# Last attention of a four-layer block: scores first in each step, three places for the weights, and the sums of weights inverted while compact

## The chip, the cores and the metric

The kernel runs on one core of a Trainium2 chip. The metric is the device time of one execution in microseconds (us). The core has five engines, each with its own instruction queue, worked off in order: PE (TensorE, matrix products; PEld are its weight loads), DVE (VectorE), ACT (ScalarE), POOL (GpSimd) and SP, which here only issues DMA transfers. Engines wait for one another on semaphores. SBUF is the on-chip memory of 128 partitions; PSUM, eight banks of 512 float32 per partition (`ps` in the code), takes PE's results.

## The reference, cut to what matters

Four layers of gated cross-attention and feed-forward act on 32 batches of 56 queries, with 1500 context rows of 96 features each. The change lies in the attention of the last layer, called L3:

```python
# 32 batches, 56 queries of 128 features, 1500 keys of 96 features, 16 heads of 8
q = (query @ Wq + bq); k = (key_value @ Wk + bk); v = (key_value @ Wv + bv)
attn = jnp.einsum('bhqd,bhkd->bhqk', q, k) * scale
attn = jnp.clip(attn, -CLAMP, CLAMP)              # CLAMP = 10000
attn = jax.nn.softmax(attn, axis=-1)
attn = jnp.where(jnp.any(jnp.isnan(attn)), 1.0 / Nkv, attn)
x = jnp.einsum('bhqk,bhkd->bqhd', attn, v)
return x @ Wo + bo
```

## The kernel before

All of L3's attention is `clipped_pass`. The 32 batches go through a pipeline in software: batches 0 to 7 and 24 to 31 are written out, 8 to 23 are two turns of a loop over eight batches (`batches`). A batch is 12 steps (`KT`), k = 0 to 11, one for each tile of 125 keys; a tile has 896 columns, 16 heads times 56 queries. Every engine has its own `body(b)`, and the order of the calls in it is the order of its queue.

**Step k of batch b** does, for the tile k of this batch, the last part of its work, and for later ones the first parts:

- PE: `weigh(b, k)` (line 1942, 8 products of the weights `P` with the values, summed in bank 4), then `chunks` (line 1910, 2 products of 500 columns for the maximum of batch b+1 or b+2, bank pair 6 and 7), then `score(b, k + 2)` (line 1929, 8 products, bank pair 0 and 1 or 2 and 3), then `fifth_bank(b, k)`.
- DVE: `chunk_max` (line 2109, the maximum over the two chunks), then `clip_tile(b, k + 2)` (line 2126), which clips scores from PSUM into a place of `P`. `P` has two places, so the clip of tile n waits until tile n-2 is weighed. In k = 2 two small operations follow the maximum (lines 2114 and 2117).
- ACT: `Exp` of tile n in place (line 2075), and ahead of it what the fifth bank holds (`empty(misc(b, n - 2))`) and, at n = 5, 7 and 8, a third of `second_of_keys` (line 2031).

**The fifth bank** of PSUM (index 5) is shared by all side work, in an order that the table `MISC` sets: keys of batch b+3 in three parts (k = 0, 1, 2; PE line 1844, emptied by ACT lines 2016 and 2020), at k = 3 in even batches the sums of the weights of the two batches before (`spread_sums`, line 1868) and in odd ones the projection (`project`, line 1877), at k = 6 the turned maximum of batch b+1 (`turn`, lines 1858 and 1859), at k = 7 to 10 the values of batch b+1 (line 1851, emptied by ACT line 2008). Before a new tenant PE waits until the last one is emptied (`used_earlier`, `emptied`).

**Sums.** `copy_sums` (ACT line 2043) brings a batch's bank 4, 128x224, to `UE`. In each even batch PE spreads the sums of the weights over the rows of their head (result 128x448), and DVE inverts them in two halves of 224 columns, at k = 3 and 4 (`invert`, line 2139). POOL multiplies (`norm`, lines 1806 and 1808).

**Keys.** They are split into three bfloat16 parts on ACT and POOL (lines 2016, 1770, 2031, 1775), and when the last third is ready SP issues six DMAs of 375 KB (`place_keys`, line 1708) into one of four buffers `KS`. `chunks` of batch b+2 needs them at step k = 3 of batch b. The turned maximum goes out and back by DMA (`place_max`, lines 1713 to 1717), ahead of the keys in SP's queue, and the first clip of the next batch waits for it.

The lines that set the order of a step before are these:

```python
for k in range(KT):                       # PE
    weigh(b, k)
    chunks(of, c)
    score(b, k + 2)
    fifth_bank(b, k)
for k in range(KT):                       # DVE
    chunk_max(of, c)
    clip_tile(b, k + 2)
    if b.r % 2 == 0 and (b - 2).there() and k in (3, 4):
        invert(b - 2, k - 3)
```

Of the kernel before, what the change touches and what calls it, by code (L numbers as in the profile page):

```python
# [15 lines left out]
BF16 = mybir.dt.bfloat16  # L16
# [17 lines left out]
DH = 8  # L34
# [1490 lines left out]
class Eight(Batch):  # L1525
# [12 lines left out]
                "u_copied", "sums_spread", "sums_inverted", "u_normed", "seen", "projected", "out_copied"]  # L1538
# [51 lines left out]
def clipped_pass(core, L, S, src, bo, scale, clip, ok, ctx):  # L1590
# [6 lines left out]
    QS = [sb(f"qs{s}", [128, HQ + 16], BF16) for s in range(8)]  # L1597
# [24 lines left out]
    def queries(b):  # L1622
        return QS[b.r % 8][:, 0:HQ].rearrange("p (m j q) -> p m j q", j=2, q=NQ)
# [24 lines left out]
    MISC = {0: ("keys", 0), 1: ("keys", 1), 2: ("keys", 2), 3: ("pair", 0), 6: ("turn", 0),  # L1648
            7: ("values", 0), 8: ("values", 1), 9: ("values", 2), 10: ("values", 3)}

    def misc(b, k):
# [3 lines left out]
        kind, n = MISC[k]  # L1655
        if kind == "pair":
            kind = "project" if b.r % 2 else "sums"
        of = {"values": b + 1, "keys": b + 3, "turn": b + 1, "sums": b - 2, "project": b - 3}[kind]
# [4 lines left out]
    def emptied(kind, n, of):  # L1663
# [26 lines left out]
    with nc.Block() as block:  # L1690
        @block.sync
        def _(sp):
# [55 lines left out]
        def _(pool):  # L1748
# [8 lines left out]
            def place_queries(b):  # L1757

                if b.turn is not None or b.r >= 8:
                    pool.wait_ge(S["scored"], b.lin(12, -84))  # L1760
                for u, (_, part) in enumerate(PRODUCTS):
                    for j in range(2):
# [3 lines left out]
                                       ).then_inc(S[f"q_in{b.r % 8}"], 16)  # L1766
# [35 lines left out]
            def norm(b):  # L1802
                pool.wait_ge(S["sums_inverted"], b.lin(1, 2))
# [23 lines left out]
            pool.wait_ge(S["q_zeroed"], 8)  # L1827
# [7 lines left out]
            place_queries(first + 3)  # L1835
# [4 lines left out]
        def _(pe):  # L1840
# [21 lines left out]
            def of_head(t, j):  # L1862
                return t.rearrange("p (s r j q) -> p (s r) j q", s=2, j=2, q=NQ)[:, :, j, :]
# [1815 lines left out]
```

## Time and profile before

| | before |
| --- | --- |
| median of 3 runs | 4645.66 us |
| lowest and highest | 4640.62 and 4651.19 us |
| the profiled execution | 4638.98 us, of it 4637.4 us span |
| L3's attention, steps of all batches | about 3580 to 4533 us of the span |
| busy in these 953 us: DVE, PE, ACT, POOL | 866, 810, 583, 465 us |
| granted TensorE clock in them | 0.94 of full |

The stage fills a fifth of the span. No engine is busy in all of it, but DVE and PE are so in over four fifths, and which of them ends a step last differs from step to step; so the rows below show single steps. A row of the timeline begins with its start in us from the span's start, then how long it took, the engine, the line, the operation and, in brackets, how long the engine was idle before it and who released it.

### The profile page before, as it was taken

To read this page: it belongs to the slowest core of one execution; us is meant where nothing else is said; L and a number is where in the kernel's file an instruction comes from. 1 tells how busy PE (TensorE), PEld (TensorE's weight loads), DVE (VectorE), ACT (ScalarE), POOL (GpSimd) and SP (SyncE) were. 2 spreads that over 40 slices of the span, in tenths; PEclk is the share of its full clock that TensorE was granted. 3 is DMA by queue.
4 is the path that set the end of the run, shared out by engine and by line. 5 is a ranking of instruction groups with operands and counts; after the bars stand their busy time and mean duration, and the time that the engine had idled before them with its cause. 6 is when DMAs were issued, how large, how long until landed. Compare 5 with 4: busy or idle time off the path is not lost. (4 is left out here: it accounts for less than half of the span.)

```text
span 4637.4 us, 86565 instructions
## 1 busy us (share of the span) xinstructions
PE 3793.5 (82%) x32862; PEld 2469.2 (53%) x32862; DVE 2849.1 (61%) x3552; ACT 2051.5 (44%) x2875; POOL 1444.6 (31%) x1905
## 2 busy tenths in 40 slices
PE   7389889871748999998999996599595888888885
PEld 7156556640425666664666663277332555555553
DVE  8666555643336555535555543577546999989993
ACT  7166666640212334332343342366222666656652
POOL 0264445303132323212223210022005555545520
PEclk9689999985868999997999997799796999989997
DMA  6166666723532323212333320110004665555630
GB/s 168 38 150 147 146 136 142 157 70 133 196 71 53 88 84 83 80 46 70 85 87 87 83 59 15 42 48 28 17 0 105 136 137 134 127 131 130 136 87 14
DMA packets 197065, 434.62 MB, mean 94 GB/s; under 512 B 45707, under 2 KB 98877, under 8 KB 196588
## 3 DMA queue, kind: packets, MB, share of 16 engines
q1 hardware_dynamic: 122196, 338.87, 28.9%
q0 software_dynamic: 38912, 47.06, 4.7%
q10 hardware_dynamic: 35616, 43.97, 3.5%
q8 instruction: 236, 3.87, 0.4%
q14 instruction: 105, 0.86, 0.1%
HBM read 244.72 MB, written 32.67 MB: 60 GB/s over the span
## 5 line engine op out<-in xcount | busy, mean ns | idle before, releaser
L1446 DVE TENSOR_REDUCE L_mp<-ps 112x2 f32<-112x1000 f32 x384 | 458.2, 1199 | 507.7 <-PE ps L1268 504.1
L1305 PE MATMUL ps<-L_p,L_cn 125*97 125x448 f32 x1536 | 639.2, 538 | 0.0
L1429 ACT ACTIVATE L_p<-ps 125x896 f32<-125x896 f32 x384 | 352.2, 917 | 612.5 <-PE ps L1293 540.5
L2109 DVE TENSOR_REDUCE L_mp<-ps 112x2 f32<-112x1000 f32 x384 | 456.6, 1193 | 71.4 <-PE ps L1910 48.3
L2075 ACT ACTIVATE L_p<-L_p 125x896 f32<-125x896 f32 x384 | 365.1, 951 | 254.9 <-DVE L_p L2126 254.6
L911 ACT ACTIVATE L_p<-ps,rk 125x896 f32<-125x896 f32 x384 | 385.8, 1005 | 161.9 <-PE ps L789 142.9
L2126 DVE SCALAR_TENSOR_TENSOR L_p<-ps,xn 125x896 f32<-125x896 f32 x384 | 415.1, 1082 | 26.6 <-DMA xn<-L_low 17.9
L1291 PE MATMUL ps<-L_qh,L_ch 97*125 97x448 f32 x768 | 385.6, 502 | 13.9 <-DMA L_qh<-L_mc 13.9
L1305 PEld LDWEIGHTS ps<-L_p,L_cn 125*97 125x97 f32 x1536 | 250.4, 163 | 205.8 <-issue 165.9
L1942 PE MATMUL ps<-L_p,L_vs 125*18 125x112 f32 x6144 | 233.6, 272 | 113.7 <-ACT L_p L2075 101.6
L1910 PE MATMUL ps<-L_ks,L_qs 96*128 96x500 bf16 x768 | 248.6, 410 | 46.2 <-DVE L_mp L2109 23.7
L1292 PE MATMUL ps<-L_ql,L_ch 96*125 96x448 f32 x768 | 283.9, 370 | 0.0
L1293 PE MATMUL ps<-L_qh,L_cl 96*125 96x448 f32 x768 | 282.2, 367 | 0.0
L1268 PE MATMUL ps<-L_cr,L_qb 96*112 96x500 f32 x768 | 269.0, 437 | 13.3 <-DVE L_mp L1446 7.0
L802 PE MATMUL ps<-L_p,L_vs 125*32 125x112 f32 x6144 | 240.1, 275 | 30.9 <-ACT L_p L911 13.0
L1942 PEld LDWEIGHTS ps<-L_p,L_vs 125*18 125x18 f32 x6144 | 131.5, 100 | 235.9 <-ACT L_p L2075 191.5
L1929 PEld LDWEIGHTS ps<-L_qs,L_ks 128*128 128x128 bf16 x3072 | 199.8, 102 | 101.8 <-issue 21.4
L789 PE MATMUL ps<-L_qs,L_ks 128*128 128x112 bf16 x3072 | 230.3, 221 | 6.1 <-issue 6.1
L1929 PE MATMUL ps<-L_qs,L_ks 128*128 128x112 bf16 x3072 | 226.9, 220 | 4.5 <-DMA L_qs<-L_mt 4.5
L710 POOL DMA_DIRECT2D L_qs<-L_q_part x384 | 216.9, 573 | 9.7 <-DVEq L1018 6.8
L1764 POOL DMA_DIRECT2D L_qs<-L_q_part x384 | 214.2, 565 | 8.1 <-issue 5.5
L1220 POOL TENSOR_TENSOR L_un<-L_ue,L_rb 96x896 f32<-96x896 f32 x32 | 67.2, 2101 | 453.9 <-DMA L_rb<-L_den 453.9
(518 smaller groups left out, 7285.5 us busy)
## 6 DMA issues: line engine op xcount, KB each, us to landing
L_ks<-L_k_part SPq DMA_DIRECT2D x288, 375.0 KB, 9.7
L_ks<-L_k_first SPq DMA_DIRECT2D x96, 375.0 KB, 7.2
moe_w<-in_L_w SPq DMA_DIRECT2D x64, 512.0 KB
L_cn<-in_ctxN SPq DMA_DIRECT2D x32, 568.4 KB
cs_ct<-in_ctxT SPq DMA_DIRECT2D x32, 562.5 KB, 4.2
L_raw<-in_ctxT SPq DMA_DIRECT2D x32, 562.5 KB
L_cr<-in_ctxT POOLq DMA_DIRECT2D x32, 562.5 KB, 4.9
L_ch<-in_ctxT POOLq DMA_DIRECT2D x32, 562.5 KB, 4.4
```

The source lines that it names most:

```text
L911: nc.scalar.activation(P[0:KP, n % 2, :].rearrange("p (a n) -> p a n", a=2), SB[n % 2][0:KP], ACT.Exp, scale=rk[:, bass.ds(b.lin(KT, n), 1 ...
L1291: nc.tensor.matmul(SB[n % 2][:, a, :], CH[s][:, k], QH[s][:, q], start=True, stop=False)
L1292: nc.tensor.matmul(SB[n % 2][:, a, :], CH[s][0:DC, k], QL[s][:, q], start=False, stop=False)
L1293: mm = nc.tensor.matmul(SB[n % 2][:, a, :], CL[s][:, k], QH[s][0:DC, q], start=False, stop=True)
L1305: mm = nc.tensor.matmul(U[:, a, :], CN[s][:, j, :], P[:, n % 2, a * HALF:(a + 1) * HALF], start=(j == 0), stop=(j == KT - 1))
L1429: nc.scalar.activation(two(P[:, n % 2, :]), SB[n % 2], ACT.Exp).then_inc(S["exped"].sem, 1)
L1446: nc.vector.tensor_reduce(mp[:, 2 * k:2 * k + 2], ps[0:TT, bank:bank + 2, 0:500], AX.X, ALU.max).then_inc(S["chunk_maxed"].sem, 1)
L1929: mm = nc.tensor.matmul(SB[n % 2][:, m // 4, m % 4 * 2 * NQ:(m % 4 + 1) * 2 * NQ] .rearrange("p (j q) -> p j q", j=2), KS[b.r % 4][:, k0:k ...
L1942: mm = nc.tensor.matmul(ps[32 * g:32 * g + VW, 4, c:c + 2 * NQ], VS[b.r % 2][:, j, m, :], P[0:KP, j % 2, m * 2 * NQ:(m + 1) * 2 * NQ], sta ...
L2075: nc.scalar.activation(two(P[0:KP, n % 2, :]), two(P[0:KP, n % 2, :]), ACT.Exp).then_inc(S["exped"], 1)
L2109: nc.vector.tensor_reduce(mp[:, 2 * c:2 * c + 2], ps[0:TT, CB[pair], 0:500], AX.X, ALU.max).then_inc(S["chunk_maxed"], 1)
L2126: nc.vector.scalar_tensor_tensor(out=two(P[0:KP, n % 2, :]), in0=SB[n % 2][0:KP], scalar=0.0, in1=two(LB[0:KP, b.r % 2, :]), op0=ALU.min, ...
```

## The change

Parts, all within `clipped_pass`:

1. PE's step begins with `score(b, k + 2)`, and `weigh`, `chunks` and `fifth_bank` follow. DVE's step begins with `clip_tile(b, k + 2)`, and `chunk_max` follows.
2. `P` has three places instead of two; to pay for them `QS`, the queries' buffers, go from eight to four, and queries are placed three batches ahead instead of four.
3. ACT empties the fifth bank one tile later (ahead of tile n what step n-3 put there, not n-2), and the first third of `second_of_keys` moves from n = 5 to 6.
4. The sums are first picked out compactly: `pick_sums` (PE, k = 3, 4 products with 4 columns) gives 112x16, `invert` is one reciprocal of 112x16, `widen` (ACT, ahead of tile 6) repeats it to two tiles 112x256, `spread_sums` (PE, k = 5, 4 products with 112 columns) brings them to 128x448, and `take_sums` (ACT, ahead of tile 8) copies that to `RD` for POOL.
5. The turned maximum moves from k = 6 to k = 4.

```diff
-    QS = [sb(f"qs{s}", [128, HQ + 16], BF16) for s in range(8)]
+    QS = [sb(f"qs{s}", [128, HQ + 16], BF16) for s in range(4)]
-    P = sb("p", [128, 2, HQ])
+    P = sb("p", [128, 3, HQ])
+    RC = sb("rc", [2 * NQ, 4, 4])
-    MISC = {0: ("keys", 0), 1: ("keys", 1), 2: ("keys", 2), 3: ("pair", 0), 6: ("turn", 0),
+    MISC = {0: ("keys", 0), 1: ("keys", 1), 2: ("keys", 2), 3: ("pair", 0), 4: ("turn", 0), 5: ("spread", 0),
...
+            def pick_sums(b):
+                pe.wait_ge(S["u_copied"], b.lin(1, 2))
+                for c in range(4):
+                    mm = nc.tensor.matmul(ps[0:2 * NQ, 5, 4 * c:4 * c + 4], UE[:, c // 2, c % 2 * 2 * NQ:][:, 0:2 * NQ],
+                                          core.ident[:, DH:128:32], start=True, stop=True)
+                mm.then_inc(S["sums_picked"], 1)
             def spread_sums(b):
-                pe.wait_ge(S["u_copied"], b.lin(1, 2))
-                for j in range(2):
-                    mm = nc.tensor.matmul(of_head(ps[:, 5, 0:2 * QV], j), core.sum_row[:, j, :],
-                                          of_head(UE[:, :, :].rearrange("p s n -> p (s n)"), j),
-                                          start=True, stop=True)
+                pe.wait_ge(S["sums_widened"], twice_half_of(b, 2))
+                for c in range(4):
+                    mm = nc.tensor.matmul(ps[:, 5, c * 2 * NQ:(c + 1) * 2 * NQ],
+                                          wide(c // 2)[:, c % 2 * 128:(c % 2 + 1) * 128],
+                                          core.ident[0:2 * NQ, 0:2 * NQ], start=True, stop=True)
...
             def body(b):            # PE
                 for k in range(KT):
+                    if k + 2 < KT:
+                        score(b, k + 2)
+                    elif (b + 1).there():
+                        score(b + 1, k + 2 - KT)
                     weigh(b, k)
                     of, c = chunk_of(b, k)
                     if of.there():
                         chunks(of, c)
-                    if k + 2 < KT:
-                        score(b, k + 2)
-                    elif (b + 1).there():
-                        score(b + 1, k + 2 - KT)
                     fifth_bank(b, k)
...
+            def widen(b):           # ACT
+                act.wait_ge(S["sums_inverted"], half_of(b, 1))
+                if b.turn is not None or b.r:
+                    act.wait_ge(S["u_normed"], b.lin(1, 0))
+                    act.wait_ge(S["projected"], half_of(b, 0))
+                for n in range(2):
+                    nc.scalar.activation(wide(n).rearrange("p (c g d) -> p c g d", c=2, g=4),
+                                         RC[:, 2 * n:2 * n + 2, :].unsqueeze(3).to_broadcast([2 * NQ, 2, 4, 32]),
+                                         ACT.Copy).then_inc(S["sums_widened"], 1)
...
-                    if n >= 2:
-                        empty(misc(b, n - 2))
+                    if n >= 3:
+                        empty(misc(b, n - 3))
                     elif (b - 1).there():
-                        empty(misc(b - 1, n + 10))
-                    for at, c in ((5, 0), (7, 1), (8, 2)):
+                        empty(misc(b - 1, n + 9))
+                    if n == 6 and b.r % 2 == 0 and (b - 2).there():
+                        widen(b - 2)
+                    for at, c in ((6, 0), (7, 1), (8, 2)):
...
             def clip_tile(b, n):    # DVE
-                if b.turn is not None or b.r or n >= 2:
-                    dve.wait_ge(S["weighed"], b.lin(12, n - 1))
+                if b.turn is not None or b.r or n >= 3:
+                    dve.wait_ge(S["weighed"], b.lin(12, n - 2))
...
-                nc.vector.reciprocal(RD[:, s, :], ps[:, 5, s * QV:(s + 1) * QV]).then_inc(S["sums_inverted"], 1)
+                nc.vector.reciprocal(RC[:, :, :].rearrange("p c g -> p (c g)"), ps[0:2 * NQ, 5, 0:16]
+                                     ).then_inc(S["sums_inverted"], 1)
             def body(b):            # DVE
                 for k in range(KT):
-                    of, c = chunk_of(b, k)
-                    if of.there():
-                        chunk_max(of, c)
                     if k + 2 < KT:
                         clip_tile(b, k + 2)
                     elif (b + 1).there():
                         clip_tile(b + 1, k + 2 - KT)
-                    if b.r % 2 == 0 and (b - 2).there() and k in (3, 4):
-                        invert(b - 2, k - 3)
+                    of, c = chunk_of(b, k)
+                    if of.there():
+                        chunk_max(of, c)
+                    if b.r % 2 == 0 and (b - 2).there() and k == 3:
+                        invert(b - 2)
```

DVE's queue in steps 2 to 5 of an even batch, before (L2109 is the maximum, L2126 the clip, L2114 and L2117 the two small operations that end a batch's maximum):

```order
L2109 TENSOR_REDUCE L_mp<-ps 112x2
L2114 TENSOR_REDUCE L_mu<-L_mp 112x8
L2117 TENSOR_SCALAR L_mc<-L_mu 112x8
L2126 SCALAR_TENSOR_TENSOR L_p<-ps,xn 125x896
L2109 TENSOR_REDUCE L_mp<-ps 112x2
L2126 SCALAR_TENSOR_TENSOR L_p<-ps,xn 125x896
L2139 RECIPROCAL L_rd<-ps 128x224
L2109 TENSOR_REDUCE L_mp<-ps 112x2
L2126 SCALAR_TENSOR_TENSOR L_p<-ps,xn 125x896
L2139 RECIPROCAL L_rd<-ps 128x224
```

The same place after the change (L2152 is the maximum, L2169 the clip):

```order
L2152 TENSOR_REDUCE L_mp<-ps 112x2
L2157 TENSOR_REDUCE L_mu<-L_mp 112x8
L2160 TENSOR_SCALAR L_mc<-L_mu 112x8
L2169 SCALAR_TENSOR_TENSOR L_p<-ps,xn 125x896
L2152 TENSOR_REDUCE L_mp<-ps 112x2
L2182 RECIPROCAL L_rc<-ps 112x16
L2169 SCALAR_TENSOR_TENSOR L_p<-ps,xn 125x896
L2152 TENSOR_REDUCE L_mp<-ps 112x2
L2169 SCALAR_TENSOR_TENSOR L_p<-ps,xn 125x896
```

Clips and maxima alternate as they did; two reciprocals of 224 columns have become one of 16.

PE's queue from step 2 of an even batch, before (L1844 keys, L1942 weigh, L1910 chunks, L1929 score, L1868 the sums spread):

```order
L1844 MATMUL ps<-L_ck,L_wk 128x500
L1942 MATMUL ps<-L_p,L_vs 18x112 x8
L1910 MATMUL ps<-L_ks,L_qs 128x500 x2
L1929 MATMUL ps<-L_qs,L_ks 128x112 x8
L1868 MATMUL ps<-L_ue,sum_row 128x4x56 x2
L1942 MATMUL ps<-L_p,L_vs 18x112 x8
L1910 MATMUL ps<-L_ks,L_qs 128x500 x2
L1929 MATMUL ps<-L_qs,L_ks 128x112 x8
L1942 MATMUL ps<-L_p,L_vs 18x112 x8
```

And after (L1857 keys, L1948 score, L1961 weigh, L1929 chunks, L1878 the sums picked, L1871 and L1872 the turned maximum, L1885 the inverted sums spread):

```order
L1857 MATMUL ps<-L_ck,L_wk 128x500
L1948 MATMUL ps<-L_qs,L_ks 128x112 x8
L1961 MATMUL ps<-L_p,L_vs 18x112 x8
L1929 MATMUL ps<-L_ks,L_qs 128x500 x2
L1878 MATMUL ps<-ident,L_ue 112x4 x4
L1948 MATMUL ps<-L_qs,L_ks 128x112 x8
L1961 MATMUL ps<-L_p,L_vs 18x112 x8
L1929 MATMUL ps<-L_ks,L_qs 128x500 x2
L1871 MATMUL ps<-ident,L_st 24x112
L1872 MATMUL ps<-ident,L_st 8x112
L1948 MATMUL ps<-L_qs,L_ks 128x112 x8
L1961 MATMUL ps<-L_p,L_vs 18x112 x8
```

The scores now stand behind the fifth bank's work and ahead of the weighing, where they stood behind the chunks.

## Rows read from the trace of the kernel before

**Rows 1.** The stage: us, busy PE, PEld, DVE, ACT, POOL; clock, DMA share, GB/s

```profile
3580.00:4533.00 953.00, 810.35 (x11074) 517.19 (x11078) 866.07 (x839) 583.16 (x877) 464.75 (x802) 0.94 0.56 126
```

**Rows 2.** Timeline of DVE: clip of tile 1 in batches 2, 13, 14, 30

```profile
3640.54 1.08 DVE L2126 SCALAR_TENSOR_TENSOR L_p<-ps,xn 125x896 f32<-125x896 f32 x1
...
3973.86 1.08 DVE L2126 SCALAR_TENSOR_TENSOR L_p<-ps,xn 125x896 f32<-125x896 f32 x1
...
4001.23 1.08 DVE L2126 SCALAR_TENSOR_TENSOR L_p<-ps,xn 125x896 f32<-125x896 f32 x1
...
4491.02 1.08 DVE L2126 SCALAR_TENSOR_TENSOR L_p<-ps,xn 125x896 f32<-125x896 f32 x1
```

**Rows 3.** Timeline, batch 14, steps 3 to 7: reciprocals and what waits

```profile
4011.83 1.08 DVE L2126 SCALAR_TENSOR_TENSOR L_p<-ps,xn 125x896 f32<-125x896 f32 x1
...
4012.83 1.55 DVE L2139 RECIPROCAL L_rd<-ps 128x224 f32<-128x224 f32 x1
...
4015.35 1.07 DVE L2126 SCALAR_TENSOR_TENSOR L_p<-ps,xn 125x896 f32<-125x896 f32 x1
...
4016.45 0.95 ACT L2075 ACTIVATE L_p<-L_p 125x896 f32<-125x896 f32 x1 [2.56 <-DVE L_p L2126]
...
4018.99 1.01 PE L1910 MATMUL ps<-L_ks,L_qs 96*128 96x500 bf16 x2 [0.59 <-DVE L_mp L2109]
...
4021.06 0.95 PE L1942 MATMUL ps<-L_p,L_vs 125*18 125x112 f32 x16
...
4024.61 0.58 PE L1942 MATMUL ps<-L_p,L_vs 125*18 125x112 f32 x16
```

**Rows 4.** Granted clock and DMA share in two stretches of batch 14, columns as in rows 1

```profile
4000.00:4004.00 4.00, 3.06 (x49) 1.78 (x51) 3.72 (x5) 2.29 (x4) 0.00 (x0) 1.00 1.05 190
...
4020.00:4024.00 4.00, 4.00 (x39) 2.71 (x37) 3.20 (x3) 2.77 (x5) 1.85 (x2) 0.51 0.03 6
```

**Rows 5.** What DVE waited for in the stage: total, times, longest

```profile
DVE L_mp L2109 <- PE ps L1910: 44.4, 75, 2.0
DVE L_p L2126 <- DMA xn<-L_low: 17.9, 10, 10.5
...
DVE L_mp L2109 <- issue: 7.9, 1, 7.9
```

**Rows 6.** Timeline, batch 14, a step with keys in the fifth bank

```profile
4003.85 0.59 ACT L2016 ACTIVATE L_k_first<-ps 128x500 bf16<-128x500 f32 x1 [0.56 <-PE ps L1844]
...
4004.34 0.58 ACT L2020 ACTIVATE L_k_full<-ps 128x500 f32<-128x500 f32 x1
...
4006.08 0.58 PE L1942 MATMUL ps<-L_p,L_vs 125*18 125x112 f32 x16
...
4007.03 0.56 PE L1929 MATMUL ps<-L_qs,L_ks 128*128 128x112 bf16 x8
...
4007.42 1.06 PE L1844 MATMUL ps<-L_ck,L_wk 97*128 97x500 f32 x2
...
4008.42 0.58 PE L1942 MATMUL ps<-L_p,L_vs 125*18 125x112 f32 x16
```

**Rows 7.** Two rows that price new operations: a DVE group, a projection

```profile
L2117 DVE TENSOR_SCALAR L_mc<-L_mu 112x8 f32<-112x8 f32 x32 | 5.5, 172 | 1.1
...
4043.51 1.10 PE L1877 MATMUL ps<-L_un,L_woe 128*128 128x112 f32 x8
```

**Rows 8.** The keys' DMAs placed in batch 13, and the chunk that waits

```profile
3992.05 1.30 SPq L1708 DMA_DIRECT2D L_ks<-L_k_first  x2
...
4010.08 0.59 PE L1910 MATMUL ps<-L_ks,L_qs 96*128 96x500 bf16 x2 [1.09 <-DMA L_ks<-L_k_part]
```

**Rows 9.** Timeline of the last steps and of the end of the stage

```profile
4526.22 1.09 DVE L2126 SCALAR_TENSOR_TENSOR L_p<-ps,xn 125x896 f32<-125x896 f32 x1 [0.80 <-PE ps L1929]
...
4529.46 1.09 DVE L2126 SCALAR_TENSOR_TENSOR L_p<-ps,xn 125x896 f32<-125x896 f32 x1 [0.79 <-PE ps L1929]
...
4535.13 2.97 DVE L2139 RECIPROCAL L_rd<-ps 128x224 f32<-128x224 f32 x2 [3.21 <-PE ps L1868]
```

More of the change, by code:

```diff
@@ L1655, in misc @@
         kind, n = MISC[k]
+        if kind == "spread" and b.r % 2:
+            return None
         if kind == "pair":
             kind = "project" if b.r % 2 else "sums"
-        of = {"values": b + 1, "keys": b + 3, "turn": b + 1, "sums": b - 2, "project": b - 3}[kind]
+        of = {"values": b + 1, "keys": b + 3, "turn": b + 1, "sums": b - 2, "spread": b - 2, "project": b - 3}[kind]
         if not of.there():
@@ L1671, in emptied @@
         if kind == "sums":
-            return S["sums_inverted"], of.lin(1, 2)
+            return S["sums_inverted"], half_of(of, 1)
+        if kind == "spread":
+            return S["sums_copied"], half_of(of, 1)
         return S["out_copied"], half_of(of, 1)
@@ L1679, in half_of, with wide, twice_half_of @@
         return 4 * b.turn + (b.r // 2 + c)
+    def wide(n):
+        return (RD, UN)[n][0:2 * NQ, :, :].rearrange("p s n -> p (s n)")[:, 0:256]
+    def twice_half_of(b, c):
+        if b.turn is None:
+            return b.r // 2 * 2 + c
+        return 8 * b.turn + (b.r // 2 * 2 + c)
     def used_earlier(b, k):
@@ L1757, in place_queries @@
             def place_queries(b):
-                if b.turn is not None or b.r >= 8:
-                    pool.wait_ge(S["scored"], b.lin(12, -84))
+                if b.turn is not None or b.r >= 4:
+                    pool.wait_ge(S["scored"], b.lin(12, -36))
                 for u, (_, part) in enumerate(PRODUCTS):
@@ L1810, in body @@
             def body(b):
-                if (b + 4).there():
-                    place_queries(b + 4)
+                if (b + 3).there():
+                    place_queries(b + 3)
                 if (b + 3).there():
@@ L1834, in _ @@
             place_queries(first + 2)
-            place_queries(first + 3)
             batches(pool, body)
@@ L1894, in fifth_bank @@
                 if kind == "sums":
+                    pick_sums(of)
+                if kind == "spread":
                     spread_sums(of)
@@ L1999, in _ @@
             pe.wait_ge(*emptied("project", 0, last - 2))
+            pick_sums(last)
             spread_sums(last)
@@ L2043, in copy_sums, with take_sums @@
                 nc.scalar.activation(UE[:, b.r % 2, :], ps[:, 4, 0:QV], ACT.Copy).then_inc(S["u_copied"], 1)
+            def widen(b):
[7 more added lines that the diff above has]
+                                         ACT.Copy).then_inc(S["sums_widened"], 1)
+            def take_sums(b):
+                act.wait_ge(S["sums_spread"], half_of(b, 1))
+                if b.turn is not None or b.r:
+                    act.wait_ge(S["u_normed"], b.lin(1, 0))
+                nc.scalar.activation(RD[:, :, :].rearrange("p s n -> p (s n)"), ps[:, 5, 0:2 * QV], ACT.Copy
+                                     ).then_inc(S["sums_copied"], 1)
             def out(b):
@@ L2059, in empty @@
                     copy_turned(of)
+                if kind == "spread":
+                    take_sums(of)
                 if kind == "project":
@@ L2074, in body @@
                     act.wait_ge(S["clipped"], b.lin(12, n + 1))
-                    nc.scalar.activation(two(P[0:KP, n % 2, :]), two(P[0:KP, n % 2, :]), ACT.Exp
+                    nc.scalar.activation(two(P[0:KP, n % 3, :]), two(P[0:KP, n % 3, :]), ACT.Exp
                                          ).then_inc(S["exped"], 1)
@@ L2100, in make_parts @@
                 dve.wait_ge(S["q_made"], 1)
-                qf, rest = (t[:, :, :].rearrange("p s n -> p (s n)") for t in (P, LB))
+                qf, rest = (t[:, :, :].rearrange("p s n -> p (s n)") for t in (P[:, 0:2, :], LB))
                 link(nc.vector.tensor_scalar(qf.rearrange("p (c n) -> p c n", c=NCH), ps[:, 0:NCH, 0:CH],
@@ L2123, in clip_tile @@
                 dve.wait_ge(S["scored"], b.lin(12, n + 1))
-                if b.turn is not None or b.r or n >= 2:
-                    dve.wait_ge(S["weighed"], b.lin(12, n - 1))
-                nc.vector.scalar_tensor_tensor(out=two(P[0:KP, n % 2, :]), in0=SB[n % 2][0:KP], scalar=0.0,
+                if b.turn is not None or b.r or n >= 3:
+                    dve.wait_ge(S["weighed"], b.lin(12, n - 2))
+                nc.vector.scalar_tensor_tensor(out=two(P[0:KP, n % 3, :]), in0=SB[n % 2][0:KP], scalar=0.0,
                                                in1=two(LB[0:KP, b.r % 2, :]), op0=ALU.min, op1=ALU.max
@@ L2167, in _ @@
             batches(dve, body)
-            for s in range(2):
-                invert(Eight(None, B - 2), s)
+            invert(Eight(None, B - 2))
             dve.wait_ge(S["u_normed"], B)
```

30 lines of the change are left out of this document (15 added, 15 removed).

## The prediction

> **What bounds the kernel now.** I read first the span by stretches, then DVE's timeline over whole batches, then single steps. In the stage DVE is busy 866 of 953 us and PE 810 [rows 1]; ACT with 583 and POOL with 465 have room. So a step ends with DVE or PE, and the question is which, step by step. One step of DVE is a clip and a maximum. Where nothing else happens they follow one another without idle time; batch 13, an odd one, runs from its clip of tile 1 at 3973.86 to that of batch 14 at 4001.23, in 27.37 us [rows 2]. Less 0.35 us for the two small operations of step 2 (0.17 each [rows 7]) that is 2.25 us a step. Over batches 2 to 29 the same measure is 4491.02 - 3640.54 = 850.5 us for 28 batches [rows 2]. In it lies one stop of 7.9 us in which DVE waited for nothing that the profile names ("issue", once) [rows 5]; it stands at the turn of the loop, the change does not touch it, and I leave it in both times. The rest, 842.6 us, is 30.1 us a batch, 2.7 more than batch 13 took. If every batch ran like batch 13, 28 x 2.72 = 76.2 us would go. That is the room I look into.
>
> **Where the room is.** In even batches DVE inverts two halves of 224 columns. One reciprocal takes 1.55 us, and it is not hidden: the clips at 4011.83 and 4015.35 stand 3.52 us apart [rows 3], against 2.25 us for a step with nothing in it, and the next pair is alike. Meanwhile ACT waits 2.56 us for its clip and PE 0.59 us for the maximum [rows 3]. So two reciprocals cost an even batch 2.5 us at once. Behind them the chunks take 1.01 us for 2 products instead of 0.59 [rows 3, 8] and the granted clock falls to 0.51 of full, the lower of its two levels (1.2 of 2.4 GHz), from 1.00 [rows 4]: ahead of it PE had had 1.7 us of work (0.58 + 0.59 + 0.56 [rows 6, 8]) in each of two steps of 3.5 us, and now its steps are longer than DVE's. The remaining excess is in waits of DVE for the chunks (44.4 us in 75 waits, the low clock among their causes) and for the returned maximum (17.9 us, of it 10.5 in the first batch) [rows 5]. In the one odd batch shown none of this happens, though its queue is else the same; this is why I take an odd batch as the model of what is left.
>
> **The change part by part.** All against the profiled execution of 4638.98 us.
>
> *The reciprocal.* It goes from 2 x 224 to 16 columns. Its price lies between 0.17 us, the group of 8 columns [rows 7], and the 16/224 of 1.55 on top of that, 0.28; I take 0.2, since the 8 columns already carry what is fixed. It waits for `pick_sums`, 4 products of 4 columns, which end while the maximum of step 3 still runs: nothing on the path. Batch 13 has no reciprocal, so against 76.2 us 14 even batches pay 14 x 0.2 = 2.8 us.
>
> *Widening, spreading, taking.* On PE, `spread_sums` is four products with 112 columns, as the projection is: 1.10 us [rows 7]; with the other three groups that makes a step of about 2.4 us, 0.15 over DVE's 2.25, so 14 x 0.15 = 2.1 us. From below it is nothing, since step 6 has no tenant and gives it back. On ACT, two copies of 256 columns cost under 0.59 each, the price of 500 [rows 6], say 0.4, and taking 448 columns about 0.55: 1.4 us in 2 batches, spread over two steps in which ACT now waits for its clip. POOL's `norm` gets its sums at tile 8 instead of step 4; it comes behind the thirds of the keys, which end about then anyway, so it costs nothing as long as those do.
>
> *Scores first, three places.* The order on DVE is as before, clip and maximum in turn, and PE does the same products a batch. In steps with side work in the fifth bank PE is itself full (a keys step is 4006.08 to 4008.42, 2.34 us, with no idle time [rows 6]), and no order changes that. So in full batches I give this nothing beyond batch 13's time. At the end of the stage it counts: from batch 30, step 3, on there are no chunks, and two steps take 4529.46 - 4526.22 = 3.24 us [rows 9], because clip, exponential, weighing and scores form a ring over two places. With three places and scores ahead of the weighing the ring opens, and a step is bound by DVE's 1.09 or PE's 0.58 + 0.56. Of 18 steps some 10 have no tenant: 10 x (1.62 - 1.12) = 5.0 us. Batch 30's own two reciprocals save 2.5 us, and 0.4 for the clock behind them. At the very end 2.97 us of reciprocals [rows 9] and a 1 us spreading turn into picking, 0.2, widening, 1.10 and taking, about 3.5 us in all: 0.4 us. Together 8.3 us.
>
> *ACT one tile later.* Here the change can lose. Before a new tenant PE waits until ACT has emptied the bank. For keys that now means: exponential of tile k+1, then two copies, 4003.85 to 4004.92, 1.07 us [rows 6], and only then the next 1.06 us of products and 0.6 of scores. Counted from DVE's clip in step 1: ACT is through with tile 2 at -0.2, with the copies at 0.9; keys to 1.95, scores to 2.6 us. DVE would be ready at 2.25, and the step takes 2.34 now. So one step in each batch grows by 0.26 us, 28 x 0.26 = 7.3 us. Step 2 hides the same behind the two small operations, step 3 behind a tenant that starts later; values are copied faster and pass. The bounds are 0 (the phase between PE and DVE takes it up) and three such steps, 22 us.
>
> *The maximum turned two steps earlier, four buffers of queries.* SP hands out the returned maximum before the keys, and the clip of the next batch has some 1 to 2 us more: the 7.4 us of waits after the first batch mostly end. They are not in batch 13, so this is already in the room. Queries are still placed more than a batch ahead of their use; nothing.
>
> *What does not go.* Batches also differ by small stalls, keys that land late above all; I leave 0.1 us a batch, 2.8 us.
>
> **The sum.** 76.2 - 2.8 - 2.1 - 7.3 - 2.8 = 61.2 us, with 8.3 at the end 69.5 us. From 4638.98 this gives 4569.5 us. The median of the three runs was 4645.66, 6.7 us above the profiled execution, and the new median should stand alike: **4576 us**.
>
> **The rivals.**
>
> *The keys' DMA becomes the bound.* The keys of batch 13 were handed out from 3992.05, and the chunk that needs them started at 4010.08, having waited 1.09 us [rows 8]: 18 us, with the DMA engines full (share 1.05 [rows 4]). After the change I put the last third at 8.9 us behind step 3's clip (three steps of 2.25, then ACT and POOL with 2.2 us), so keys allow a period of 27 us; DVE needs 27.6. Against: the margin is positive. For: it is 0.6 us, and I take one burst for all. Each us beyond costs 28 us; at one, 4604 us.
>
> *ACT holds up the fifth bank in more steps.* If keys, projection and values each lose 0.2 to 0.3 us, 1 us a batch, the time is again 4604 us.
>
> *The low clock stays.* If steps 4 to 6 of even batches, where PE works 1.7 of 2.25 us, are enough to bring it down without the reciprocals, about 2 us in 14 batches remain: 28 us, 4604 us. Against it is batch 13, which has such steps at full clock.
>
> *More than I allow.* Without the losses of ACT and spreading, and with stalls gone, 12 to 15 us more go: 4562 us.
>
> *Slower than before.* One mechanism: the clock. PE's waits for ACT in steps 1 and 3 are new idle times, in every batch and not in every second. Should they bring the clock down, a step costs 3.55 us (4021.06 to 4024.61 [rows 3]) instead of 2.25, 1.3 more. The gain is used up when 69.5 / 1.3 = 53 of the 336 steps run so in addition, 16%; the granted clock in the stage would fall from 0.94 [rows 1] to under 0.90. At 25% of the steps, 84 of them, the time is 4576 + 84 x 1.3 = 4685 us. Against it: a keys step of 2.6 us still holds 2.3 us of PE's work, where ahead of the fall two steps of 3.5 us held 1.7 each. The Trainium skill (TensorE: Matmul & The Clock Gate, section "A second HAM failure mode: psum-queue depth-cycling") reports a kernel that cycled through PSUM banks and left PE idle briefly between groups so often that the clock went up and down, at a price in throughput. This trace agrees in part: the fall in batch 14 came behind idle times, but odd batches with shorter ones stay at full clock.
>
> *The change does not free DVE.* Excluded by the 3.52 us, in which DVE has no idle time.
>
> **How the numbers follow.** Forecast 62% (4576, within 12 either way); more 7%; keys' DMA 9%; ACT 9%; low clock stays 8%; slower 4%; a mixture that nets to nothing 1%. The range, 4552 to 4608 us, takes in the deeper gain and the three at 4604. A measurement of this kernel tells about 0.2%, 9 us, from no change: faster 0.94, same 0.02, slower 0.04.
>
> **What would show it.** Even and odd batches alike, both about 27.6 us; clips 2.2 to 2.5 us apart around the small reciprocal, which takes 0.2; the granted clock in the stage at 0.97 or more; ACT no longer waiting 2.5 us. The keys step 1 to 2 grows to about 2.6 us if the ACT term is right. The last steps come at 1.1 us. The DMA rival would show as chunks released by the keys in most batches, the ACT rival as keys and values products released by its copies with DVE idle after, the clock rival as chunks of 1.01 us. A mean batch above 28.5 us would make the prediction wrong.

## The result, and the profile after

The changed kernel takes 4528.81 us (median of 4 runs, 4514.69 to 4530.06), the kernel before, beside it, 4645.25 us. That is 116 us less; the ratio is 0.974, 95% interval 0.9723 to 0.9757. Forecast were 4576 us, 69 us less, with a range down to 4552. The sign was right; the gain is 1.7 times the forecast one, and the time lies outside the range.

The profiled execution has a span of 4528.5 us, 108.9 less than before. Measured as in [rows 2], from the clip of tile 1 in batch 2 to that in batch 30, the steps take 749.1 us instead of 850.5: 101.4 of the 108.9 us are there. The sum had 61.2 for them. It had 8.3 for the end of the stage, where 4.3 us went: the clips of batches 30 and 31 are through 4.9 us sooner, and the work behind the last clip takes 0.6 us longer. Batches 0 and 1, which the sum left out, gave 6.1 us, and the work outside the stage took 2.8 us more. So the error is in the full batches. Two equal stretches of the stage show the pace; the first line of numbers is after, the second before (columns as in [rows 1]):

```profile
3640.00:4300.00 660.00, 611.31 (x8749) 414.13 (x8748) 636.38 (x654) 461.70 (x740) 390.46 (x668) 0.99 0.67 151
```

```profile
3640.00:4300.00 660.00, 565.65 (x7525) 357.84 (x7529) 601.56 (x584) 404.28 (x615) 340.18 (x580) 0.93 0.58 133
```

DVE is now busy 96% of the time, and the granted clock is 0.99. An even batch takes 26.29 us and an odd one 26.21, almost without spread but for batches 15 and 16 at the turn of the loop (34.6 and 32.3 us). The forecast had 27.6 for both, because it took the 27.37 us of batch 13 [rows 2] for what is left when the reciprocals go.

The groups of the stage after, 3580 to 4440 us, as in [rows 7] (busy, mean ns, idle before):

```profile
L2152 DVE TENSOR_REDUCE L_mp<-ps 112x2 f32<-112x1000 f32 x363 | 432.0, 1190 | 2.6 <-PE ps L1929 2.6
L2169 DVE SCALAR_TENSOR_TENSOR L_p<-ps,xn 125x896 f32<-125x896 f32 x384 | 414.5, 1081 | 40.5 <-PE ps L1948 29.1 <-DMA xn<-L_low 11.0
L2116 ACT ACTIVATE L_p<-L_p 125x896 f32<-125x896 f32 x384 | 364.7, 950 | 228.0 <-DVE L_p L2169 227.4
```

The maximum waits 2.6 us for its chunks where it waited 44.4 [rows 5], and of the 40.5 us ahead of the clip 11.0 are the first batch and 8.3 + 3.2 the stop at the turn of the loop. No instruction of the stage waited for the keys' DMAs any more.

**How a step ran before and runs now.** Timeline of the kernel before, batch 15, steps 4 and 5, with no tenant (no side work) in the fifth bank:

```profile
4046.81 1.08 DVE L2126 SCALAR_TENSOR_TENSOR L_p<-ps,xn 125x896 f32<-125x896 f32 x1
...
4047.81 1.19 DVE L2109 TENSOR_REDUCE L_mp<-ps 112x2 f32<-112x1000 f32 x1
4047.93 0.95 ACT L2075 ACTIVATE L_p<-L_p 125x896 f32<-125x896 f32 x1 [1.42 <-DVE L_p L2126]
...
4048.91 1.08 DVE L2126 SCALAR_TENSOR_TENSOR L_p<-ps,xn 125x896 f32<-125x896 f32 x1
4048.93 0.58 PE L1942 MATMUL ps<-L_p,L_vs 125*18 125x112 f32 x16 [0.87 <-ACT L_p L2075]
4049.44 0.60 PE L1910 MATMUL ps<-L_ks,L_qs 96*128 96x500 bf16 x2
...
4050.07 1.20 DVE L2109 TENSOR_REDUCE L_mp<-ps 112x2 f32<-112x1000 f32 x1
...
4051.19 1.08 DVE L2126 SCALAR_TENSOR_TENSOR L_p<-ps,xn 125x896 f32<-125x896 f32 x1
```

DVE seems busy without a gap, yet the second maximum starts 1.16 us after its clip and the first 1.00. The second one waited: the chunks end at 4049.44 + 0.60 = 4050.04, and it starts at 4050.07. The records of two successive DVE instructions overlap by 0.08 us (1.08 long, 1.00 apart), and idle time as short as the other 0.08 us here is not printed, so a wait of 0.16 us shows neither as idle time nor as a releaser. From this follows a ring, a chain of waits that comes back to where it began, through DVE, ACT and PE: clip at 4046.81, exponential at 4047.93, weighing at 4048.93, chunks, maximum at 4050.07, clip at 4051.19. That is 4.38 us for two steps, 2.19 a step, where DVE alone would take 2.10. The same in the changed kernel, batch 14:

```profile
3974.57 1.08 DVE L2169 SCALAR_TENSOR_TENSOR L_p<-ps,xn 125x896 f32<-125x896 f32 x1
...
3974.71 0.60 PE L1929 MATMUL ps<-L_ks,L_qs 96*128 96x500 bf16 x2 [0.39 <-DVE L_mp L2152]
...
3975.57 1.19 DVE L2152 TENSOR_REDUCE L_mp<-ps 112x2 f32<-112x1000 f32 x1
...
3975.89 0.56 PE L1948 MATMUL ps<-L_qs,L_ks 128*128 128x112 bf16 x8
...
3976.37 0.58 PE L1961 MATMUL ps<-L_p,L_vs 125*18 125x112 f32 x16
...
3976.68 1.08 DVE L2169 SCALAR_TENSOR_TENSOR L_p<-ps,xn 125x896 f32<-125x896 f32 x1
...
3976.89 0.60 PE L1929 MATMUL ps<-L_ks,L_qs 96*128 96x500 bf16 x2
```

Clip to maximum is 1.00 us, maximum to clip 1.11: 2.10 us a step, and this is a step with values in the fifth bank, which took 2.23. Here PE waits for DVE (0.39), not the other way. From then on PE is slower than DVE as long as the fifth bank has values: its chunks are 2.18 us apart (3974.71, 3976.89), the clips 2.11 (3974.57, 3976.68). PE enters these steps with a lead, loses some 0.07 us in each, and has it again from steps without a tenant, where its chunks come as close as 1.89 us apart. The clip at 3976.68 starts while the tile two before it is still being weighed (3976.37 to 3976.95), which needs the third place.

### The profile page after: what moved, and what is told of

Same layout as the page of the kernel before. It is cut to its first block and busy times, and to the rows that moved or that the text cites. A ratio compares the mean times of both kernels' runs of the same rounds, so it can differ in the third digit from the quotient of the medians.

```text
span 4528.5 us, 87018 instructions
## 1 busy us (share of the span) xinstructions
PE 3764.9 (83%) x33054; PEld 2482.9 (55%) x33054; DVE 2775.7 (61%) x3532; ACT 2053.0 (45%) x2923; POOL 1442.9 (32%) x1905
## 5 line engine op out<-in xcount | busy, mean ns | idle before, releaser
L2152 DVE TENSOR_REDUCE L_mp<-ps 112x2 f32<-112x1000 f32 x384 | 455.4, 1190 | 6.5 <-PE ps L1929 6.5
L2169 DVE SCALAR_TENSOR_TENSOR L_p<-ps,xn 125x896 f32<-125x896 f32 x384 | 414.5, 1081 | 40.5 <-PE ps L1948 29.1
L1929 PE MATMUL ps<-L_ks,L_qs 96*128 96x500 bf16 x768 | 236.2, 392 | 62.4 <-DVE L_mp L2152 50.6
L802 PE MATMUL ps<-L_p,L_vs 125*32 125x112 f32 x6144 | 240.8, 275 | 32.2 <-ACT L_ue L895 19.9
L1948 PEld LDWEIGHTS ps<-L_qs,L_ks 128*128 128x128 bf16 x3072 | 190.2, 99 | 90.2 <-issue 54.0
L789 PE MATMUL ps<-L_qs,L_ks 128*128 128x112 bf16 x3072 | 228.8, 220 | 6.9 <-issue 6.9
L1948 PE MATMUL ps<-L_qs,L_ks 128*128 128x112 bf16 x3072 | 216.5, 214 | 14.7 <-DVE L_p L2169 6.5
L1961 PE MATMUL ps<-L_p,L_vs 125*18 125x112 f32 x6144 | 223.7, 263 | 1.4 <-ACT L_p L2116 0.9
L789 PEld LDWEIGHTS ps<-L_qs,L_ks 128*128 128x128 bf16 x3072 | 166.1, 101 | 77.9 <-issue 70.7
```

The source lines that it names most:

```text
L789: mm = nc.tensor.matmul(SB[n % 2][:, m // 4, m % 4 * 2 * NQ:(m % 4 + 1) * 2 * NQ] .rearrange("p (j q) -> p j q", j=2), KS[b.r % 3][:, k0:k ...
L1948: mm = nc.tensor.matmul(SB[n % 2][:, m // 4, m % 4 * 2 * NQ:(m % 4 + 1) * 2 * NQ] .rearrange("p (j q) -> p j q", j=2), KS[b.r % 4][:, k0:k ...
L2152: nc.vector.tensor_reduce(mp[:, 2 * c:2 * c + 2], ps[0:TT, CB[pair], 0:500], AX.X, ALU.max).then_inc(S["chunk_maxed"], 1)
L2169: nc.vector.scalar_tensor_tensor(out=two(P[0:KP, n % 3, :]), in0=SB[n % 2][0:KP], scalar=0.0, in1=two(LB[0:KP, b.r % 2, :]), op0=ALU.min, ...
```

## The experiments

All times are medians beside runs of the kernel before on the same chip, and the ratio is to these. "Odd" and "even" are the median batches among 2 to 29 of the profiled execution, clip of tile 1 to clip of tile 1; all kernels keep the computation whole. The edits below are cut to the lines that matter, with calls shortened.

| run | us | ratio, 95% interval | odd, even batch | clock 3640 to 4300 |
| --- | --- | --- | --- | --- |
| before | 4645.25 | 1 | 27.8, 32.6 | 0.93 |
| after | 4528.81 | 0.974, 0.9723 to 0.9757 | 26.2, 26.3 | 0.99 |
| dve_order | 5029.80 | 1.0831, 1.081 to 1.0853 | 43.3, 42.6 | 0.80 |
| pe_order | 4631.81 | 0.9968, 0.9956 to 0.9981 | 27.2, 31.9 | 0.94 |
| both_orders | 4656.91 | 1.0034, 1.0019 to 1.0049 | 28.1, 32.2 | 0.93 |
| small_sums | 4588.46 | 0.9877, 0.986 to 0.9895 | 28.0, 28.4 | 0.98 |
| both_orders_small_sums | 4611.55 | 0.9923, 0.99 to 0.9946 | 28.6, 29.2 | 0.97 |
| small_sums_three_places | 4598.67 | 0.9909, 0.989 to 0.9927 | 28.1, 28.4 | 0.98 |
| after_two_places | 4603.09 | 0.9912, 0.9894 to 0.993 | 28.2, 28.6 | 0.99 |
| after_wide_sums | 4592.96 | 0.989, 0.9869 to 0.991 | 26.5, 30.1 | 0.94 |
| after_late_turn | 4647.37 | 1.0012, 0.9997 to 1.0026 | 30.8, 30.7 | 0.91 |
| after_again | 4529.92 | 0.9758, 0.974 to 0.9775 | 26.2, 26.3 | 0.99 |
| after_early_empty | 4514.30 | 0.9727, 0.9707 to 0.9748 | 25.9, 26.0 | 0.99 |
| early_empty_again | 4511.59 | 0.9721, 0.9704 to 0.9738 | 25.9, 26.0 | 0.99 |

**The sums alone.** The kernel before with part 4 only; the spreading at step 5, the turned maximum left at 6.

```diff
-    MISC = {..., 3: ("pair", 0), 6: ("turn", 0),
+    MISC = {..., 3: ("pair", 0), 5: ("spread", 0), 6: ("turn", 0),
-                    if b.r % 2 == 0 and (b - 2).there() and k in (3, 4):
-                        invert(b - 2, k - 3)
+                    if b.r % 2 == 0 and (b - 2).there() and k == 3:
+                        invert(b - 2)
```

> The kernel before with only the sums changed (picked, inverted as 112x16, widened, spread at step 5, taken by ACT); order, places and the turned maximum at step 6 stay. If the forecast's reading of the reciprocals was right, even batches come down from 32.3 to 27.5 to 28.0 us and odd ones stay at 27.4 to 27.7: 14 x 4.5 + 3 = 66 us less, about 4579 us, and the granted clock in the stage rises from 0.94 to 0.97 or more. If the low clock does not come from the reciprocals, about 38 us less and a clock of 0.95.

It took 4588.46 us, 56 less. Even batches fell from 32.6 to 28.4 us, odd ones stayed at 28, and the clock rose to 0.98:

```profile
3640.00:4300.00 660.00, 581.96 (x8165) 379.11 (x8164) 609.20 (x610) 440.64 (x688) 363.77 (x620) 0.98 0.62 142
```

So the forecast's reading of the reciprocals holds, the clock included, with 56 instead of 66 us; between 3640 and 4300 us DVE's waits for the chunks (30.1 us) and for the returned maximum (7.5 us) remain. What is left, 60 us, the forecast had given almost nothing.

**DVE's order alone.**

```diff
-                    chunk_max(of, c)                # DVE
-                    clip_tile(b, k + 2)
+                    clip_tile(b, k + 2)
+                    chunk_max(of, c)
```

> The kernel before with one edit: in DVE's step the clip of tile k+2 stands ahead of the maximum of step k; PE's order, two places of weights and the wide reciprocals stay. Theory A (a ring through DVE's order: clip n, exponential n, weighing n, chunks n, maximum n, clip n+2; 1.08 + 0.04 + 0.95 + 0.05 + 0.51 + 0.60 + 0.03 + 1.12 = 4.38 us in two steps, 2.19 a step): the ring is opened by this edit alone, an odd batch falls from 27.4 to about 26.5 us, the maximum follows the clip after 1.00 instead of 1.11 to 1.22 us; some 25 us less than the kernel before. Theory B (PE's order alone makes the step shorter, since the scores move behind the fifth bank's work): no change within 5 us, odd batches stay at 27.4.

385 us slower. I had followed the ring of two steps and overlooked that this edit closes one within a single step. Its timeline, in steps with keys:

```profile
4145.86 0.60 PE L1910 MATMUL ps<-L_ks,L_qs 96*128 96x500 bf16 x2
4146.30 0.56 PE L1929 MATMUL ps<-L_qs,L_ks 128*128 128x112 bf16 x8
...
4146.89 1.09 DVE L2126 SCALAR_TENSOR_TENSOR L_p<-ps,xn 125x896 f32<-125x896 f32 x1 [1.09 <-PE ps L1929]
...
4147.90 1.19 DVE L2109 TENSOR_REDUCE L_mp<-ps 112x2 f32<-112x1000 f32 x1
...
4149.15 0.60 PE L1910 MATMUL ps<-L_ks,L_qs 96*128 96x500 bf16 x2 [0.88 <-DVE L_mp L2109]
```

Chunks wait for the last maximum, scores stand behind the chunks, the clip waits for the scores and the maximum stands behind the clip: 4149.15 - 4145.86 = 3.29 us in a step at full clock, and 3.9 to 4.05 in steps at the lower clock level. Neither theory foresaw it.

**PE's order alone.**

```diff
-                    weigh(b, k); chunks(of, c); score(b, k + 2)     # PE
+                    score(b, k + 2); weigh(b, k); chunks(of, c)
```

> The kernel before with one edit: in PE's step the scores of tile k+2 stand first, ahead of weighing and chunks; DVE's order and all else stay. Theory A: the ring through the maximum stays, odd batches 27.2 us or more, no gain in full batches; only the last steps without chunks gain up to 5 us. Theory B: most of what dve_order does not give, odd batches 26.5 us, some 25 us less.

13 us less, and odd batches of 27.19 us. Theory A is right in that steps without a tenant stay at 2.19: the ring through the maximum is untouched. It is not right that full batches gain nothing: 10.5 of the 13 us are there (840.0 instead of 850.5 from batch 2 to 30), in steps with keys (2.28 instead of 2.34) and with values (2.17 to 2.21 instead of 2.23), where PE does the same products in less time.

**Both orders.**

> The kernel before with both new orders (scores first on PE, clip first on DVE), but two places of weights, eight query buffers, the fifth bank emptied as before and the wide reciprocals. Theory A: like dve_order and 5 us more at the end, about 30 us less than the kernel before, even batches still 4 to 5 us longer than odd ones. If the third place is needed for the new order, nothing is gained here, since the clip of tile n+2 waits until tile n is weighed and now comes half a step earlier.

12 us slower. Of what was expected the last sentence came true: DVE's clip is now released by the weighing. Its waits between 3640 and 4300 us, total, times and longest:

```profile
DVE L_p L2126 <- PE ps L1942: 36.5, 62, 1.8
DVE L_p L2126 <- DMA xn<-L_low: 14.2, 15, 1.9
```

**Both orders and the sums.**

> The kernel before with both new orders and the new sums, but two places of weights, eight query buffers, the fifth bank emptied as before and the maximum turned at step 6. The orders alone gained nothing (both_orders: odd batches 28.1 us). If sums and orders are independent, even batches fall to 28.3 us: 57 us less than both_orders, about 4600 us. If the orders only pay once no reciprocal stands in DVE's queue, 4560 us or less.

45 us less than both_orders, about what the sums save alone (56). The orders pay nothing with either kind of sums, so it is not the reciprocals alone that held them back. Both kernels still turn the maximum at step 6.

**The third place taken away from the changed kernel.**

```diff
-    P = sb("p", [128, 3, HQ])
+    P = sb("p", [128, 2, HQ])
...
-                if b.turn is not None or b.r or n >= 3:
-                    dve.wait_ge(S["weighed"], b.lin(12, n - 2))
+                if b.turn is not None or b.r or n >= 2:
+                    dve.wait_ge(S["weighed"], b.lin(12, n - 1))
```

> The changed kernel with two places of weights instead of three. Theory: in the changed kernel the clip of tile k+2 starts while tile k is still being weighed (3987.26 against 3987.05 to 3987.63), so with two places it must wait for the weighing, and maximum, chunks, tenant, scores, weighing, clip form a ring of two steps: 1.19 + 0.04 + 0.44 + 0.88 + 0.50 + 0.62 + 1.00 = 4.67 us with values in the fifth bank, 2.33 a step instead of 2.10, and more with keys. About 1.5 us a batch, some 42 us more than the changed kernel, 4571 us. Rival: the place only matters at the end of the stage, under 8 us more.

74 us more than the changed kernel, more than the 42 of the theory, by the mechanism named; 59 of them are in the steps of batches 2 to 29:

```profile
DVE L_p L2169 <- PE ps L1961: 56.8, 117, 7.6
```

```profile
3984.64 0.58 PE L1961 MATMUL ps<-L_p,L_vs 125*18 125x112 f32 x16
...
3985.36 1.09 DVE L2169 SCALAR_TENSOR_TENSOR L_p<-ps,xn 125x896 f32<-125x896 f32 x1 [0.33 <-PE ps L1961]
```

(The clip's start lies 0.14 us behind the modelled end of the weighing at 3985.22.) Odd batches take 28.2 us, 2 us more, where I had 1.5: steps with values alternate between 2.5 and 2.15 us as worked out, and those with keys take 2.6.

**The third place alone.** small_sums with three places and four query buffers, old order.

> The run small_sums (4588 us) with three places of weights and four query buffers added, old order on PE and DVE. Theory: with the old order the clip of tile n+2 stands behind the maximum of step n, which waits for the chunks, which stand behind the weighing of tile n; so the place is free by then anyway and the third one gains nothing in full batches: odd batches stay at 27.6 to 28.1 us, 4588 us within 6. Rival: the third place alone is what was worth 75 us in after_two_places, then 4540 us or less.

4598.67 us against 4588.46, measured on different chips and 4 us beyond the 6 expected; the steps of batches 2 to 29 take 806.6 us against 804.3. So with the old order the third place is worth nothing in full batches. The orders and the place gain only together, and, as after_late_turn shows below, only with the early turn.

**The wide reciprocals put back into the changed kernel.**

```diff
-    MISC = {..., 3: ("pair", 0), 4: ("turn", 0), 5: ("spread", 0),
+    MISC = {..., 3: ("pair", 0), 5: ("turn", 0),
-                        invert(b - 2)
+                        invert(b - 2, k - 3)        # k = 3 and 4
```

> The changed kernel with the old sums (spread at step 3, two reciprocals of 128x224 at steps 3 and 4), the maximum turned at step 5. The reciprocals cost 14 x 2.7 = 38 us in even batches. If the low clock behind them comes from them whatever the order, another 14 x 1.5 = 20 us, together about 4588 us, and chunks of 1.01 us appear in even batches only; if it came from the old order, 4568 us.

64 us more than the changed kernel, 5 us from the first theory. The clock falls to 0.94 with the new order too, and scores of 0.95 us, at the lower level, stand right behind the second reciprocal:

```profile
3941.35 1.55 DVE L2138 RECIPROCAL L_rd<-ps 128x224 f32<-128x224 f32 x1
...
3941.49 0.60 PE L1909 MATMUL ps<-L_ks,L_qs 96*128 96x500 bf16 x2 [1.89 <-DVE L_mp L2108]
...
3943.21 0.95 PE L1928 MATMUL ps<-L_qs,L_ks 128*128 128x112 bf16 x8
```

It also turns the maximum one step later, and odd batches wait about 1 us for its return; between 3640 and 4300 us that is 10.5 us in 13 waits, so some 0.4 us a batch, about 12 of the 64 us, belong to that.

**The maximum turned late.**

```diff
-    MISC = {..., 4: ("turn", 0), 5: ("spread", 0),
+    MISC = {..., 5: ("spread", 0), 6: ("turn", 0),
```

> The changed kernel with the maximum turned at step 6 instead of 4. In after_wide_sums (step 5) odd batches wait 1.0 us for the returned maximum, at step 4 nothing is waited for. If each step of delay of 2.1 us goes straight to the first clip of the next batch, this costs 3.1 us a batch, 28 x 3.1 = 87 us over the changed kernel: 4615 us. If there is slack in the return, 30 us or less.

118 us more than the changed kernel: the whole gain. The wait for the return takes 58.2 us in 21 batches between 3640 and 4300 us, and behind it comes a second cost:

```profile
DVE L_p L2169 <- DMA xn<-L_low: 58.2, 21, 4.1
```

```profile
4014.08 1.09 DVE L2169 SCALAR_TENSOR_TENSOR L_p<-ps,xn 125x896 f32<-125x896 f32 x1 [2.78 <-DMA xn<-L_low]
...
4016.34 0.76 PE L1929 MATMUL ps<-L_ks,L_qs 96*128 96x500 bf16 x2 [2.54 <-DVE L_mp L2152]
...
4018.66 1.02 PE L1929 MATMUL ps<-L_ks,L_qs 96*128 96x500 bf16 x2
```

PE stands idle for 2.5 us, then its scores take 0.95 us and the chunks 1.02, the lower level, so that a batch loses more behind the wait: 2.3 us in batch 13 (steps of 3.60 and 3.31 instead of 2.10 and 2.51), 0.5 in batch 14 and 1.4 on average. The expectation had the first cost, 87 us, without the second.

**ACT empties the bank as early as before.**

```diff
-                    if n >= 3:
-                        empty(misc(b, n - 3))
+                    if n >= 2:
+                        empty(misc(b, n - 2))
...
```

> The changed kernel with ACT emptying the fifth bank ahead of tile n what step n-2 put there, as the kernel before does. Theory A (the forecast's term for ACT): the stall of 0.40 us between the clips of steps 1 and 2 goes, 9 us less than the changed kernel, about 4520 us. Theory B: the exponentials now wait behind products that are made late in the step, weighing and chunks wait for them, and steps with tenants grow: 10 us more or worse.

4514.30 us, 14.5 less than the changed kernel had. To be sure of so little, both ran again side by side:

> The changed kernel once more, as the partner of early_empty_again on the same chip: 4515 to 4531 us, ratio to the kernel before 0.974.

> The changed kernel with the fifth bank emptied one tile earlier (as after_early_empty, a second time beside after_again). The step from 1 to 2 took 2.18 us in it instead of 2.50, so 28 x 0.33 = 9 us less than after_again, and 2 us more at the ends: 4515 us when after_again has 4526. If the 14 us between the first measurements were a matter of the chip, no difference.

4529.92 and 4511.59 us, 18 us apart. Theory A holds: the clips of steps 1 and 2 are 2.18 us apart instead of 2.50, and nothing is lost elsewhere. In the changed kernel, batch 14, the second clip waits for its scores:

```profile
3960.97 1.08 DVE L2169 SCALAR_TENSOR_TENSOR L_p<-ps,xn 125x896 f32<-125x896 f32 x1
...
3963.47 1.09 DVE L2169 SCALAR_TENSOR_TENSOR L_p<-ps,xn 125x896 f32<-125x896 f32 x1 [0.32 <-PE ps L1948]
```

In after_early_empty the clip no longer has a releaser:

```profile
3925.29 1.08 DVE L2169 SCALAR_TENSOR_TENSOR L_p<-ps,xn 125x896 f32<-125x896 f32 x1
...
3927.47 1.09 DVE L2169 SCALAR_TENSOR_TENSOR L_p<-ps,xn 125x896 f32<-125x896 f32 x1
```

The 0.32 us a batch make 9 us in 28 batches; the steps of batches 2 to 29 gave 13.9 (749.1 against 735.2 us). The other 5 are at the turn of the loop, where batches 15 and 16 together take 66.9 us in the changed kernel and 61.4 here. First the changed kernel, then after_early_empty:

```profile
4014.98 1.80 PE L1864 MATMUL ps<-L_wve,L_cv 97*125 97x144 f32 x6 [6.95 <-ACT L_vs L2028]
...
4017.57 1.09 DVE L2169 SCALAR_TENSOR_TENSOR L_p<-ps,xn 125x896 f32<-125x896 f32 x1 [8.28 <-PE ps L1948]
...
4022.88 0.92 PE L1948 MATMUL ps<-L_qs,L_ks 128*128 128x112 bf16 x8 [3.52 <-issue]
...
4023.84 1.09 DVE L2169 SCALAR_TENSOR_TENSOR L_p<-ps,xn 125x896 f32<-125x896 f32 x1 [3.24 <-PE ps L1948]
```

```profile
4007.17 0.93 PE L1948 MATMUL ps<-L_qs,L_ks 128*128 128x112 bf16 x8 [7.47 <-issue]
...
4008.14 1.09 DVE L2169 SCALAR_TENSOR_TENSOR L_p<-ps,xn 125x896 f32<-125x896 f32 x1 [7.19 <-PE ps L1948]
```

With the later emptying PE first waits 6.95 us for ACT, which stands at its own turn of the loop, and comes to its own stop of 3.52 us only after that; with the early one the two stops overlap. This is read from these two traces, and no run was made for it.

This version, the changed kernel without the later emptying, beats both: 0.972 of the kernel before. Its odd batch of 25.86 us is 12 steps of 2.10 and 0.45 for the two small operations, 25.65, and 0.2 more: what is left is DVE's own work.

## Why the prediction was wrong

**The step that failed** is the model of what is left: "If every batch ran like batch 13, 28 x 2.72 = 76.2 us would go. That is the room I look into", and with it "So in full batches I give this nothing beyond batch 13's time". Batch 13 was read as DVE at its pace because its clips and maxima stand without idle time. They did not run at DVE's pace: 2.19 to 2.23 us a step instead of 2.10. In steps without a tenant the ring over exponential, weighing, chunks and maximum set it. In steps with values PE was taken to be full at 2.23 us; with the scores placed behind the tenant the same products follow at 2.17, and what is left of PE's excess over DVE is carried from step to step by the lead that three places allow. What went was 850.5 - 749.1 = 101.4 us, more than the 76.2 before anything was subtracted. Of the 40 us between 61.2 and 101.4, the pace makes 28 x (27.37 - 26.25) = 31 us; that pace already holds what the changed kernel does lose in every batch, so the 15 us subtracted for losses come on top, and some 6 us went the other way, at the turn of the loop. The prediction left 7.9 us there in both times, but batches 15 and 16 exceed two median batches by 14.4 us now (10.2 before).

**The reciprocals, right.** One 112x16 takes 0.25 us (0.2 forecast), an even batch is 0.08 us longer than an odd one, and the sums alone gave 56 us. Put back, they cost 64, some 12 of it by the later turn. That the low clock stems from them is shown from both sides: 0.98 without them in the old order, 0.94 with them in the new.

**Spreading on PE, right in its lower bound.** 2.1 us were charged; in the steps with it the clips stay within 2.11 us of one another.

**The end of the stage, too high.** 8.3 us were credited and 4.3 went. Of the 18 steps from batch 30, step 3, on, 8 take 1.01 to 1.10 us as forecast, but others up to 2.68. The work behind the last clip grew by 0.6 us instead of shrinking by 0.4: picking took 0.92 us (as in full batches, where it delays nothing) for the 0.2 of the forecast, and spreading, at the lower clock level, 2.05 for 1.10.

**ACT one tile later, right in mechanism, too small in size.** 2.6 us were forecast between the clips of steps 1 and 2, 2.50 measured, against 2.18 without it: 9 us in 28 batches where 7.3 were charged. Undoing it gave 14.5 and 18 us, since it also sets ACT's stop and PE's at the turn of the loop one behind the other (5 us), which the forecast did not see. This part of the change lost time.

**The turned maximum, mis-sized.** It was called "already in the room". At the old pace it was. At the new one the steps get shorter and the return does not: from the issue of the outgoing transfer to the first clip it is 8.8 us (median) in after_late_turn and 9.0 in small_sums. With the turn at step 6 it costs 118 us. The gain of the orders exists only with it.

**The third place.** It was credited at the end of the stage alone. Together with the orders it carries 74 us, 59 of them in the steps of batches 2 to 29.

**The rivals.** Keys' DMAs did not become the bound: no wait is left, though the DMA share rose to 0.67. The low clock did not stay. In full batches the clock did not fall behind PE's waits for ACT (0.99). "More than I allow" had the right direction with 4562 us, and stopped at the same floor.

The Trainium skill (TensorE: Matmul & The Clock Gate, "A second HAM failure mode: psum-queue depth-cycling") speaks of short idle times between groups that make the clock go up and down. In the changed kernel the 85 waits of PE's chunks for DVE between 3640 and 4300 us, up to 0.6 us long, left it at 0.99, so that rule did not bite there. It fell behind single waits of 1.9 us (after_wide_sums) and 2.5 us (after_late_turn), and in the kernel before behind shorter ones, in the two steps of 3.5 us with the reciprocals; there the trace agrees with the page:

```profile
4013.95 0.58 PE L1942 MATMUL ps<-L_p,L_vs 125*18 125x112 f32 x16 [0.62 <-ACT L_p L2075]
...
4015.49 0.60 PE L1910 MATMUL ps<-L_ks,L_qs 96*128 96x500 bf16 x2 [0.96 <-DVE L_mp L2109]
...
4017.46 0.95 PE L1942 MATMUL ps<-L_p,L_vs 125*18 125x112 f32 x16 [0.97 <-ACT L_p L2075]
```

What was not tried: each of the two orders with three places and the early turn, which would price them one by one, and the early turn with the old orders. What it could give there is small by an estimate from small_sums, whose waits for the return are 7.5 us between 3640 and 4300 us, and the ring of 2.19 us a step would stay. A cost for a single part is not given here, since the parts hold one another up: any one of three taken away from the changed kernel costs 64, 74 or 118 us, and their sum is over twice the gain.

## What to carry to other kernels

The fastest stretch of a trace is not a floor: compare the start-to-start distances of the same two instructions and take the shortest as the engine's pace, for a short wait can leave no idle time in what the timeline prints. A ring of engines is opened by order, by a buffer more and by an earlier start of what comes back over DMA, and half of that can cost more than nothing (0.3% slower with both orders, 8% with one of them). When a pace rises, look again at every transfer of fixed length, and at each part of a change that delays something (here the later emptying), for it may be the one to leave out.

## What the runs showed of the hardware

Two successive DVE instructions overlap in the records by 0.08 us: a clip of 1.08 us is followed by the maximum after 1.00. A wait of 0.16 us was invisible there. And in after_late_turn waits of PE of 1.9 to 3 us at the first clip of a batch were followed by products at the lower clock level (scores of 0.95 us instead of 0.56): on top of 2.6 us of waiting a batch lost 1.4 us more on average.
